# One layer of gated cross-attention and a mixture of experts: attention scores in row tiles

## What is computed

```
x = x + tanh(g_xattn) * attention(layernorm(x), ctx, ctx, mask)   # 16 heads of 8
    q, k, v = projections with bias; scores = q k^T / sqrt(8), masked
    out = softmax(scores) v, merged over heads, @ Wo.T + bo
x = x + tanh(g_ffn) * experts(layernorm(x))      # 8 experts, 128 -> 512 -> 128
    gates = softmax - sigmoid threshold, kept where >= 0, divided by their sum
```

## Time and profile before

| what | us |
|---|---|
| median of three runs | 675.88 (674.58 to 676.32) |
| the profiled execution | 674.14 |
| its span, first to last instruction | 672.3 |
| TensorE busy | 639.3 (95%) |
| weight loads busy | 486.5 (72%) |
| VectorE busy | 543.5 (81%) |
| ScalarE busy | 434.3 (65%) |
| GpSimd busy | 186.2 (28%) |

### The profile page before, as it was taken

How to read it: one execution, slowest core, us unless ns; L and a number is a source line. 1 busy time by engine, 2 the same in 40 slices (tenths; PEclk the granted TensorE clock), 3 DMA queues, 4 the chain that set the end, 5 groups by cost and what they waited for, 6 DMA issues and landing times.

```text
span 672.3 us, 14393 instructions
## 1 busy us (share of the span) xinstructions
PE 639.3 (95%) x3988; PEld 486.5 (72%) x3988; DVE 543.5 (81%) x1088; ACT 434.3 (65%) x764; POOL 186.2 (28%) x240
## 2 busy tenths in 40 slices
PE   7899999999999999739999999999999999999997
PEld 6566666767766666427878878788788788787886
DVE  6788888889888888345888888888888888888886
ACT  4566666666666666417766766667667667676663
POOL 7334444444444442100221221211212212212121
PEclk9999999999999999959999999999999999999999
DMA  4544444444444444104111112112121121121120
GB/s 128 149 125 122 122 121 121 121 121 121 126 122 126 117 109 110 42 0 77 49 45 62 44 48 63 48 47 62 47 62 47 47 62 47 47 62 47 47 62 16
DMA packets 39887, 52.80 MB, mean 79 GB/s; under 512 B 9520, under 2 KB 23728, under 8 KB 39856
## 3 DMA queue, kind: packets, MB, share of 16 engines
q1 hardware_dynamic: 39856, 52.42, 28.2%
HBM read 26.58 MB, written 2.23 MB: 43 GB/s over the span
## 4 chain that ended last, share of the span: by engine, by line
PE 86%; DVE 7%; DMA 2%; issue 2%; ACT 2%; SPq 1%; POOL 0%; DVEq 0%; ACTq 0%; POOLq 0%
PE ps_h L1114 9%; PE ps_y L1094 9%; PE ps_y L1095 9%; PE ps_y L1096 9%; PE ps_h L1116 9%; PE ps_h L1115 9%; PE scores L1042 5%; PE scores L1043 4%; PE scores L1050 4%; PE scores L1051 3%; PE heads L1061 3%; DVE neg_max L681 3%; PE misc L926 2%; PE misc L927 2%; PE misc L928 2%
## 5 line engine op out<-in xcount | busy, mean ns | idle before, releaser
L645 ACT ACTIVATE h_sb<-ps_h,b_sb 128x512 f32<-128x512 f32 x256 | 176.3, 690 | 109.1 <-PE ps_h L1116 95.6
L870 DVE TENSOR_TENSOR h_low<-h_sb,h_high 128x512 fp32r<-128x512 f32 x256 | 164.3, 682 | 0.0
L866 DVE CAST h_high<-h_sb 128x512 fp32r<-128x512 f32 x128 | 98.5, 769 | 68.6 <-ACT h_sb L645 68.6
L536 POOL TENSOR_TENSOR yT<-yT,weighted 128x512 f32<-128x512 f32 x54 | 69.7, 1291 | 301.3 <-DVE weighted L858 301.3
L1114 PE MATMUL ps_h<-x_high,w_high 128*128 (+1 forms) x256 | 103.2, 403 | 1.7 <-ACT h_sb L645 1.6
L1094 PE MATMUL ps_y<-h_high,w_high 128*128 128x512 f32 x256 | 101.6, 397 | 0.8 <-DVE h_low L870 0.8
L1095 PE MATMUL ps_y<-h_low,w_high 128*128 128x512 f32 x256 | 101.5, 396 | 0.0
L1096 PE MATMUL ps_y<-h_high,w_low 128*128 128x512 f32 x256 | 101.1, 395 | 0.0
L1115 PE MATMUL ps_h<-x_low,w_high 128*128 (+1 forms) x256 | 100.3, 392 | 0.0
L1116 PE MATMUL ps_h<-x_high,w_low 128*128 (+1 forms) x256 | 100.2, 391 | 0.0
L681 DVE TENSOR_REDUCE neg_max<-scores 128x4 f32<-128x512 f32 x128 | 83.4, 685 | 10.2 <-PE scores L1051 9.3
(11 more groups left out here) (133 smaller groups left out, 1007.0 us busy)
## 6 DMA issues: line engine op xcount, KB each, us to landing
w_row<-w_scratch SPq DMA_DIRECT2D x64, 256.0 KB, 3.1
k_masked<-k_stack SPq DMA_DIRECT2D x64, 128.0 KB, 2.4
k_cur<-k_stack SPq DMA_DIRECT2D x16, 512.0 KB, 3.0
q_masked<-q_stack SPq DMA_DIRECT2D x64, 96.0 KB
w_raw<-in_w_ffn SPq DMA_DIRECT2D x16, 256.0 KB, 2.7
ctx_sb<-in_ctx SPq DMA_DIRECT2D x16, 128.0 KB, 2.1
out_y<-y_out SPq DMA_DIRECT2D x7, 256.0 KB, 2.3
x_all<-in_x SPq DMA_DIRECT2D x13, 128.0 KB, 2.4
```

Source lines behind the costliest of these rows:

```text
L645: nc.scalar.activation(h_sb[:, j % HBUF, :], ps_h[:, j % 4, :], ACT.Gelu_apprx_tanh, bias=b1_sb[:, j:j + 1]).then_inc(h_done, 1)
L866: V.tensor_copy(h_high[:, j % HBUF, :], h_sb[:, j % HBUF, :]).then_inc(high_odd, 1)
L870: V.tensor_tensor(h_low[:, j % HBUF, :], h_sb[:, j % HBUF, :], h_high[:, j % HBUF, :].bitcast(F32), ALU.subtract).then_inc(low2_done, 1)
```

## The change

Keys and queries are projected once, two outputs of 128 x 256 for a group (`kq`), with the rows in the order block, feature, slab. ScalarE writes the high part with the bias added (`kq_high`), VectorE the low part (`kq_low`). SyncE stores each part into a DRAM tensor `kq_dram`, once or twice: six transfers of 128 partitions of 1 KB, so that the rows lie threefold there. Eight transfers, each of 24 rows of 4 KB, load them into `k_st` and `q_st`, which have two buffers by the group's parity. `k_masked`, `q_masked`, `k_cur`, `part` and the stacks are gone. The bias comes by eight small transfers that ScalarE's queue issues at the start; its weights are picked from the threefold ones by a strided view.

`natural` and `transposed` are now, for each sequence, 16 matmuls with 24 or 26 rows, 128 stationary and 128 moving columns; the four row blocks stand in four row tiles of 32 and write to four banks. The mask is then added to two banks, which are handed on, and later to the other two (`natural_rest`, `transposed_rest`). `scores` has six banks: the natural ones use 0 to 3, the transposed ones 2 to 5. `misc` has two banks, which also take the values' products; the tensor `heads` is gone. VectorE takes maxima of 1024 columns, ScalarE exponentials of 1024. The maxima's rows go in four transfers per group instead of two. There is one mask copy, most buffers are doubled, all orders are new, the groups' distances are larger (`FIRST` -6, `LAST` NG + 3), and every turn is written out. Removed lines are left out below except at the top; what stood there is in the code above.

```diff
-BANKS = [["p45", "inputs", "x2T", "p01"],
-         ["p67", "max0", "p23"],
-         ["v", "heads", "merged", "gate", "wo"]]
-AHEAD = {"p45": 1, "p67": 1, "v": 1, "inputs": 2, "x2T": -1, "max0": 1, "heads": 0,
-         "p01": 2, "merged": 0, "p23": 2, "gate": -1, "wo": 0}
-FIRST, LAST = -3, NG
-STEADY = (2, NG - 5)
+BANKS = [["merged", "wo", "kq", "V1", "v", "gate", "max1"], ["x2T", "V0", "max0", "inputs", "heads"]]
+AHEAD = {"merged": -2, "x2T": -3, "wo": -2, "V0": -1, "kq": 2, "max0": 0, "inputs": 3, "V1": -1, "v": 1, "gate": -4, "heads": -1, "max1": 0}
+FIRST, LAST = -6, NG - 1 + 4
...
-        k_masked = sa("k_masked", [P, ROWS, SLABS, GT], F32R)
-        q_masked = sa("q_masked", [P, ROWS, SLABS, GT], F32R)
-        k_stack = sa("k_stack", [P, SLABS, GT], F32R)
-        q_stack = sa("q_stack", [P, SLABS, GT], F32R)
-        k_cur = sa("k_cur", [P, SLABS, GT], F32R)
...
+        k_st = sa("k_st", [P, 2, SLABS, GT], F32R)
+        q_st = sa("q_st", [P, 2, SLABS, GT], F32R)
+        kq_high = sa("kq_high", [P, 2, 2, GT], F32R)
+        kq_low = sa("kq_low", [P, 2, 2, GT], F32R)
...
-        scores = psum_a.enter_context(nc.psum_tensor("scores", [P, 4, 512], F32))
-        misc = psum_a.enter_context(nc.psum_tensor("misc", [P, 3, 512], F32))
-        heads = psum_a.enter_context(nc.psum_tensor("heads", [P, GB, GT], F32))
+        scores = psum_a.enter_context(nc.psum_tensor("scores", [P, 6, 512], F32))
+        misc = psum_a.enter_context(nc.psum_tensor("misc", [P, 2, 512], F32))
...
+        kq_dram = nc.dram_tensor("kq_scratch", (NG, 2, ROWS * 24, SLABS * GT), F32)
...
+            def store(n, c, src, g, done):
+                sp.dma_start(high_v[g, n, c], src.bitcast(F32)).then_inc(done, 16)
...
+                if (g := group_at(it, -1)) is not None:
+                    u = g % 2
+                    misc_wait_read(sp, "max1", g)
+                    wait_count(sp, tr_low_full, 2 * (g - 2) + 2)
+                    for n in range(2):
+                        sp.dma_start(q_st[24 + n::32, u, :, 1 * S:(1 + 1) * S].bitcast(F32), maxT[n * H:(n + 1) * H, 1, :].bitcast(F32)).then_inc(max_in[1][u], 16)
                 if (g := group_at(it, 1)) is not None:
...
+                if (g := group_at(it, 0)) is not None:
+                    u = g % 2
+                    misc_wait_read(sp, "max0", g)
+                    wait_count(sp, tr_low_full, 2 * (g - 2) + 1)
+                    for n in range(2):
+                        sp.dma_start(q_st[24 + n::32, u, :, 0 * S:(0 + 1) * S].bitcast(F32), maxT[n * H:(n + 1) * H, 0, :].bitcast(F32)).then_inc(max_in[0][u], 16)
+                if (g := group_at(it, 1)) is not None:
+                    u = g % 2
+                    if g == 0:
+                        sp.wait_ge(pad_done, 1)
+                    sp.wait_ge(high_stored[u], g // 2 * 64 + 64)
+                    sp.wait_ge(low_stored[u], g // 2 * 32 + 32)
+                    wait_count(sp, tr_low_full, 2 * (g - 2) + 2)
                     for r in range(ROWS):
...
+                        sp.dma_start(k_st[32 * r:32 * r + 24, u, :, :].rearrange("p s t -> p (s t)").bitcast(F32),
+                                     kq_dram[g, 0, 24 * r:24 * r + 24, :]).then_inc(km_in[u], 16)
+                    if g == 0:
+                        sp.wait_ge(pad_done, 1)
+                    sp.wait_ge(high_stored[u], g // 2 * 64 + 64)
+                    sp.wait_ge(low_stored[u], g // 2 * 32 + 32)
+                    wait_count(sp, tr_low_full, 2 * (g - 2) + 2)
                     for r in range(ROWS):
...
+                if (g := group_at(it, 2)) is not None:
+                    u = g % 2
+                    sp.wait_ge(kq_high_done, g + 1)
+                    for n, c in ((0, 0), (0, 2), (1, 0), (1, 1)):
+                        store(n, c, kq_high[:, u, n, :], g, high_stored[u])
+            loop(body)
...
+            def exps(g, b, half):
+                act.wait_ge(tr_rest_full if half else tr_low_full, 2 * g + b + 1)
...
+                nc.scalar.activation(probs[:, b, half * 8 * S:(half + 1) * 8 * S], scores[:, 2 + 2 * half:4 + 2 * half, :].rearrange("p r x -> p (r x)"),
+                                     ACT.Exp, scale=SCALE).then_inc(tr_rest_read if half else tr_low_read, 1)
...
+                        act.wait_ge(bias_in, 2 * ROWS * 16)
+                    misc_wait_full(act, "kq", g)
+                    wait_count(act, high_stored[u], g // 2 * 64)
+                    for n in range(2):
+                        ins = nc.scalar.activation(kq_high[:, u, n, :], misc[:, bank_of("kq"), n * GT:(n + 1) * GT], ACT.Identity,
+                                                   bias=bkq[:, n:n + 1])
+                    ins.then_inc(kq_high_done, 1)
...
+            def maxima(g, b, half):
+                dve.wait_ge(nat_low_full if half else nat_rest_full, 2 * g + b + 1)
+                rows = slice(2 * half, 2 * half + 2)
+                nc.vector.tensor_reduce(neg_max[:, b, rows, :], scores[:, rows, :].rearrange("p r (s k) -> p r s k", k=S),
+                                        AX.X, ALU.max, negate=True).then_inc(nat_low_read if half else nat_rest_read, 1)
...
+                    for n in range(2):
+                        ins = nc.vector.scalar_tensor_tensor(kq_low[:, u, n, :], misc[:, bank_of("kq"), n * GT:(n + 1) * GT], bkq[:, n:n + 1],
+                                                             kq_high[:, u, n, :].bitcast(F32), ALU.add, ALU.subtract)
+                    ins.then_inc(misc_read[bank_of("kq")], 1)
...
+            def natural(g, b, u):
+                if g == 0:
+                    pe.wait_ge(const_act, 2)
...
+                wait_count(pe, nat_rest_read, 2 * g + b)
+                wait_count(pe, nat_low_read, 2 * g + b)
+                wait_count(pe, tr_low_read, 2 * g - 1 + b)
+                for s in range(SLABS):
+                    for r in range(ROWS):
+                        rows = slice(32 * r, 32 * r + 24)
+                        mm(scores[:, r, s * S:(s + 1) * S], q_st[rows, u, s, b * S:(b + 1) * S], k_st[rows, u, s, b * S:(b + 1) * S],
+                           start=(s == 0), stop=False)
+                natural_mask(2, b, u)
+                natural_mask(3, b, u).then_inc(nat_low_full, 1)
...
+            def transposed(g, b, u):
+                pe.wait_ge(max_in[b][u], g // 2 * 32 + 32)
+                pe.wait_ge(nat_low_read, 2 * g + 2 if b == 0 else min(2 * g + 3, 2 * NG))
+                wait_count(pe, tr_low_read, 2 * g + b)
+                wait_count(pe, tr_rest_read, 2 * g + b)
+                for s in range(SLABS):
+                    for r in range(ROWS):
+                        rows = slice(32 * r, 32 * r + 26)
+                        mm(scores[:, 2 + r, s * S:(s + 1) * S], k_st[rows, u, s, b * S:(b + 1) * S], q_st[rows, u, s, b * S:(b + 1) * S],
+                           start=(s == 0), stop=False)
+                transposed_mask(0, b, u)
+                transposed_mask(1, b, u).then_inc(tr_low_full, 1)
...
+                if (g := group_at(it, 0)) is not None:
+                    u = g % 2
+                    natural(g, 0, u)
...
+                if (g := group_at(it, -1)) is not None:
+                    u = g % 2
+                    values(g, 0, u)
...
+                        dst = misc[:, bank_of("kq"), n * GT:(n + 1) * GT]
+                        src_h, src_l = inT_high[:, u, n * GT:(n + 1) * GT], inT_low[:, u, n * GT:(n + 1) * GT]
+                        mm(dst, wqk_high[:, n, :], src_h, start=True, stop=False)
+                        mm(dst, wqk_high[:, n, :], src_l, start=False, stop=False)
+                        ins = mm(dst, wqk_low[:, n, :], src_h, start=False, stop=True)
+                    ins.then_inc(misc_full[bank_of("kq")], 1)
+                if (g := group_at(it, -1)) is not None:
+                    u = g % 2
+                    transposed(g, 1, u)
+                if (g := group_at(it, 0)) is not None:
+                    pe.wait_ge(max_done[0], g + 1)
+                    misc_wait_free(pe, "max0", g)
+                    nc.tensor.transpose(misc[0:2 * H, bank_of("max0"), 0:S], max_parts[:, 0, :].bitcast(F32), ident[:]).then_inc(misc_full[bank_of("max0")], 1)
+                if (g := group_at(it, -1)) is not None:
+                    u = g % 2
+                    transposed_rest(g, 1, u)
...
+                if (g := group_at(it, 0)) is not None:
+                    u = g % 2
+                    natural(g, 1, u)
+                if (g := group_at(it, -1)) is not None:
+                    u = g % 2
+                    values(g, 1, u)
+                if (g := group_at(it, 0)) is not None:
+                    u = g % 2
+                    natural_rest(g, 1, u)
...
```

More of the change, by code:

```diff
@@ L989, in body @@
[L989 to L992 removed]
+                    u = g % 2
+                    transposed(g, 0, u)
+                    transposed_rest(g, 0, u)
+                if (g := group_at(it, -4)) is not None:
```

(6 more changed lines are left out.)

941 lines of the change are left out of this document (409 added, 532 removed).

## The result

The changed kernel takes **702.42 us** (median of 4 runs, 699.56 to 705.99) against 675.23 for the kernel before (4 runs beside them): ratio 1.041, interval 1.0365 to 1.0446. Slower, as forecast, by 27 us where 10 were forecast. The span of the profiled execution is 704.1 us, against 672.3.

What follows compares the result with a forecast made beforehand. TensorE bounds the old kernel; a loop through SyncE's loads was to set the beat after: 27 + 15 x 16.2 + 22.3 + 389.95 = 682.3 us span, predicted 686 median; 8-in-10 range 647 to 716, own range 678 to 700.

Steps and rivals of the forecast that it cites:

- 2.4 from its issue to landing: Transfers on SyncE's queue: 2.4 us from issue to landing, used for the stores at the start and the loop's last load.
- What goes: Attention work per group: VectorE falls to 11.9 us or less, ScalarE to 7.7 or less, TensorE's sum to 12.6.
- The score tiles: TensorE's 64 score tiles a group: 2.0 us at the value products' pace, 7.0 if one after the other.
- The queue of SyncE: SyncE's 22 transfers a group: issues rise from 9 to about 15 us, making the queue late next.
- loads 0.78: SyncE's eight 24-row loads: issues 0.78 us apart, chosen from a range of 0.40 to 0.78; 6.2 us in sum.
- cheap issues: Rival: SyncE's loads from DRAM cost 0.40 us each, loop 13.4, beat 13.8, span 643, median 647; chance 0.34.
- The loop that I expect to set the beat: TensorE to first maxima, SyncE's transfers, eight loads, next group's natural scores: 16.2 us a turn, TensorE idle some 3.
- behind these loads: SyncE's mask load and four high stores, queued after the eight loads: keep SyncE busy into the next turn.
- few DMA engines: Rival: a four-block store runs on four DMA engines, 1.9 us each; loop 18.5 us, 17.3 at 1.5; chance 0.17.
- Start 27: Start of the kernel: first natural scores at 27 us instead of 19.12, or 24 with cheap issues.
- Its clock still full: Sign for the forecast: TensorE idle 10% or more while its clock stays full.
- End: After natural(15, 0): 22.3 us to the last heads' transposes, then 389.95 us as before.

Runs made afterwards that it cites:

- the fastest version: 32-block stores, bias loads on SyncE and the mask's early load, plus the start's orders changed (fills, group loads, wqk_low); 655.98 us, ratio 0.9726 to the kernel before.
- tiles on one block: On the run with 32-block stores and bias loads on SyncE, every score tile reads rows of the first 32-row block; 811.56 us, ratio 1.2026.
- 32-block stores: The changed kernel with rows in the DRAM copy reordered so a store's DRAM side has 32 blocks instead of four; 684.81 us, ratio 1.0188.
- With the stores and bias loads mended: The changed kernel with 32-block stores and the eight bias loads moved from ScalarE's to SyncE's queue; 682.65 us, ratio 1.0144.
- with the mask early: 32-block stores and bias loads on SyncE, with the mask's load moved to the start of SyncE's turn; 661.42 us, ratio 0.9793.
- the run with the loads first: 32-block stores, bias loads on SyncE and the mask's early load, with the eight loads put ahead of the first maxima's rows; 696.38 us, ratio 1.0362.

## Why the prediction was right or wrong

The direction was right, and 702 lies inside the wide range of 647 to 716. It lies outside the forecast's own 678 to 700, and the slowing was 27 us where 10 were forecast. The step that failed is the stores' way to DRAM, "2.4 from its issue to landing": it took 8.7 us. In its own steps:

- **"What goes": right for VectorE and ScalarE, too high for TensorE.** VectorE is busy 10.7 us a turn (at most 11.9 forecast), ScalarE 7.4 (7.7). TensorE is busy 14.3, where 12.6 was the sum and 16.1 the value before; in the fastest version, at a clock of 0.99, it is 13.2. So of the 3.8 us a turn 1.8 came in the changed kernel and 2.9 in the fastest. The 3.8 had also counted 0.4 of stalls as work: 16.0 - 12.6 is 3.4.
- **"The score tiles": right** in kind, 2.4 us a group (64 x 37 ns) where 2.0 was taken from the values' tiles; 7.0, the upper end, is what tiles on one block cost, as that run shows. A tile's weight load is by its record as long as a full-height one (L889: median 187 ns for 24 rows, 0.19 us for 128), but the starts are 37 ns apart, so the loads overlap.
- **"The queue of SyncE", the term "loads 0.78": wrong.** "Row count is what separates the costly from the cheap rows" was the choice; the 24-row loads from DRAM cost 0.365, like the mask's load (0.403). The maxima cost 0.56 and the stores 0.54, where 0.73 and 0.70 were taken. With the context's 0.469 for the four plain loads, the queue's 22 issues are 2.9 + 3.2 + 2.2 + 1.9 = 10.2 us by these medians, and 11.3 us a turn by the sum of all records from 60 to 240 us, not 15.1. The premise of the rival "cheap issues" was therefore true, and its result was not: only with the stores, the mask and the start mended is its beat near (14.45 against 13.8, span 656.3 against 643).
- **"The loop that I expect to set the beat": not what set it in the changed kernel.** The sign asked for, that the first tiles of each turn wait for k_st or q_st, is seen once from 60 to 240 us (2.2 us), and the chain goes through the context's load, behind the stores. That 16.96 is near 16.2 is therefore luck in part: with issues at 0.40 to 0.45 the text's own sum of the loop is 13.4, and what the stores and the mask added took the place of the dear issues. Once the stores and the mask's load are mended the loop does set the beat, with loads of 3.3 us instead of 5.46 and a landing of 3.8 instead of 2.4. Between the two stands a link that the text put "behind these loads" and thought harmless: the mask's load (3 us and a copy), 8.0 us between the profiles in the changed kernel and 17.7 with the stores mended.
- **"2.4 from its issue to landing", for the stores: the step that failed most.** In the start it was 8.7. The rival "few DMA engines" had it, with a chance of 0.17: its 713 is near the span of 704, its beat of 17.3 to 18.5 just above 16.96, and its cause is shown by the 32-block stores, its 1.9 us a store by the start. But its sum also held issues of 0.78, so that its number comes out is luck in part. Its place was wrong: it had TensorE wait longest for the maxima's rows, which cost 3.6 us, while the context cost 21.6. The argument against it, that an idle engine may be quicker, had no row.
- **"Start 27": wrong by 12.7.** The first projection came at 18.4, not 10.3 (8.1: the text changed six stores and nothing of the orders that hold the first turns, x of group 1, v_pad's fills and the weights); the stores landed 6.4 late beyond that; the cheap loads gave 1.8 back. The eight bias loads, priced at 0.4 each, took 6.28 us on ScalarE's queue. The runs took 5.6 off by the stores, 1.5 more by the bias loads and 3.6 by the orders. What is left, 29.3, is 2 us above 27, and 5 above the 24 that the text gave for cheap issues, which is the fair comparison; 3.7 of it is the first projection, which still comes at 14.0. The cause of that stays open.
- **"Its clock still full": wrong.** 0.89. TensorE is idle 28.5 of the 180 us from 60 to 240 us, 2.7 a turn. With the stores and bias loads mended it is idle 23.3 at a clock of 0.93, with the mask early 17.1 at 0.97, in the fastest version 15.5 at 0.99. But the run with the loads first is idle 21.6 at 0.90, and the run on one block 2.8 at 0.77, so idle time alone does not tell the clock. In the changed kernel a batch's value products take 1.08 us in some turns and 1.87 in others. TensorE's busy time of a turn, 14.3 us here and 13.2 in the fastest version, puts the clock at about 1 us of the beat, an estimate from these two windows; no run took clock and waits apart.
- **"End" and the experts: right** within 1.6 us.

So the smaller work promised 3.8 us a turn, 60 us in all; TensorE's busy time fell by about half of that (1.8 us a turn), and its idle time rose from 0.3 to 2.7 us a turn. The idle time hangs on transfers, of which the two largest (four-block stores, the mask's place) were not in the change's sum; the longer start and end come on top.

## What to carry to other kernels

When work moves from an engine to a round trip through DRAM, price the round trip first: for each transfer how many blocks its slowest dimension has on both sides, and for each turn the last transfer that the next turn's first matmul needs, with everything issued in order ahead of it. A store over four blocks costs its own time and that of everyone queued behind it, so before a wait at a harmless load (here the context) is blamed on that load, look at what is queued ahead of it. And if a limit is removed and little comes, look at the next link and remove both: the mask's move was worth 8.0 us alone and 17.7 behind the stores' mending (4.7 and 21.2 by the medians).

## What the runs showed of the hardware

- A load from DRAM into 24 partitions of 4 KB rows costs its queue 0.365 us; a store from 128 partitions 0.54; a transfer from on-chip rows to q_st 0.56 (medians). But the eight bias loads, also from DRAM and 0.1 KB each, took 6.28 us on ScalarE's queue, 0.79 each, and 5.86 on SyncE's, 0.73 each: that the source is DRAM does not by itself make an issue cheap.
- The same store, 128 KB: the last of six in a row landed 8.7 us after its issue with four blocks on the DRAM side, within 2.5 with 32 blocks. With four blocks that is 1.9 us a store.
- A queue's issues can slow down while another queue issues. At the start of the changed kernel SyncE's mask load takes 0.67 us (at 5.03, first row of its timeline) while ScalarE issues its eight bias loads (0.73 to 7.01), and wo_sb's 0.43 after them; SyncE's first four issues, also beside them, take 0.45 to 0.54. With the bias loads on SyncE the mask's load takes 0.43:

```profile
4.14 0.43 SPq L333 DMA_DIRECT2D mask_words<-in_mask  x1
```

- Row tiles of 24 or 26 rows with 128 columns on four blocks run at 37 ns each, a third of the 0.12 us that they take on one block; at the lower clock one block takes 0.23.
